# Who issues the small transfer of row maxima: ScalarE's queue or the sync queue

## The reference, cut to what matters

```python
q = heads(x @ Wq + bq); k = heads(c @ Wk + bk); v = heads(c @ Wv + bv)   # 16 heads of 16 channels
att = softmax(q @ k.T / sqrt(16))            # 512 x 512 for every head
y   = att @ v
```

## Time and profile before

| | |
|---|---|
| median of 3 runs | 1839.13 us (1838.22 to 1843.45) |
| span of the profiled execution, first to last instruction | 1831.7 us |
| what lies around the span, against the median | 7.4 us |
| PE busy | 1634.0 us, 89% |
| DVE busy | 1353.5 us, 74% |
| ACT busy | 1151.3 us, 63% |
| POOL busy | 658.3 us, 36% |
| q1 (SP's queue) | 156.43 MB, 30.8% of the 16 DMA engines' time |
| q10 (ACT's queue) | 1.18 MB, 0.3% |

### The profile page before, as it was taken

One profiled execution on the slowest core, in us unless ns is written; L12 is line 12 of the kernel. 1 busy time (PEld: TensorE's weight loads), 2 busy tenths in 40 slices (PEclk: granted clock), 3 DMA queues, 4 the chain that ended last, 5 costly groups with the idle time before them and its releaser, 6 DMA issues.

```text
span 1831.7 us, 29160 instructions
## 1 busy us (share of the span) xinstructions
PE 1634.0 (89%) x10051; PEld 735.1 (40%) x10064; DVE 1353.5 (74%) x2549; ACT 1151.3 (63%) x2178; POOL 658.3 (36%) x915
## 2 busy tenths in 40 slices
PE   5897879998999989998999999988999998899677
PEld 1343335433543435433543344433543543333236
DVE  6677677788588777778687777877488687688287
ACT  1474576566755686667765685657655854756497
POOL 3422524550445234641454135622562242310140
PEclk7898989999999999999999999999999998899899
DMA  7333412323243323332242323332332231124123
GB/s 196 101 108 108 121 35 72 99 79 90 63 117 79 93 59 99 88 101 67 67 113 62 91 77 92 86 102 76 82 105 59 54 102 47 44 77 138 46 70 116
DMA packets 106947, 159.49 MB, mean 87 GB/s; under 512 B 20656, under 2 KB 83248, under 8 KB 106800
## 3 DMA queue, kind: packets, MB, share of 16 engines
q1 hardware_dynamic: 101904, 156.43, 30.8%
q10 hardware_dynamic: 4896, 1.18, 0.3%
HBM read 105.00 MB, written 51.38 MB: 85 GB/s over the span
## 4 chain that ended last, share of the span: by engine, by line
PE 54%; DVE 19%; ACT 10%; POOL 7%; issue 4%; DMA 3%; SPq 1%; ACTq 0%; DVEq 0%; POOLq 0%
PE acc L1492 11%; PE st L1478 10%; PE misc L1457 10%; DVE nmax L1255 8%; PE misc L1432 7%; PE misc L1404 4%; PE misc L1519 3%; PE misc L1444 3%; ACT probs L988 3%; ACT tail_h L1058 2%; ACT tail_h L1043 1%; PE misc L1546 1%; PE misc L1533 1%; POOL parts L873 1%; POOL qk L869 1%
## 5 line engine op out<-in xcount | busy, mean ns | idle before, releaser
L1255 DVE TENSOR_REDUCE nmax<-misc 128x1 f32<-128x512 f32 (+2 forms) x1376 | 863.8, 671 | 301.9 <-PE misc L1457 181.4
L988 ACT ACTIVATE probs<-st 128x512 f32<-128x512 f32 (+3 forms) x1536 | 760.4, 551 | 375.2 <-PE st L1478 241.3
L1457 PE MATMUL misc<-stack 96*128 96x512 bf16 (+3 forms) x1536 | 535.1, 364 | 58.2 <-DVE nmax L1255 41.1
L1478 PE MATMUL st<-stack 99*128 99x512 bf16 (+3 forms) x1536 | 539.8, 362 | 37.6 <-ACT probs L988 31.5
L1478 PEld LDWEIGHTS st<-stack 99*128 99x128 bf16 x1536 | 148.7, 98 | 377.8 <-ACT probs L988 222.0
L1457 PEld LDWEIGHTS misc<-stack 96*128 96x128 bf16 x1536 | 151.9, 99 | 199.1 <-DVE nmax L1255 83.1
L1492 PE MATMUL acc<-probs,v_x 128*32 128x512 f32 x1152 | 157.8, 621 | 0.0
L867 POOL TENSOR_TENSOR parts<-qk,zero 128x512 bf16<-128x512 f32 x78 | 81.3, 1043 | 207.6 <-ACT qk L971 207.6
L879 POOL TENSOR_TENSOR nparts<-nmax,zero 128x16 bf16<-128x16 f32 x96 | 21.3, 222 | 273.3 <-DVE nmax L1255 273.3
L1492 PE MATMUL acc<-probs,v_s 128*32 128x512 f32 (+3 forms) x1152 | 113.6, 466 | 0.1
L1481 PE MATMUL st<-mask_st,identb 128*128 128x128 bf16 x512 | 111.1, 220 | 0.0
(11 more groups left out here) (258 smaller groups left out, 2087.2 us busy)
## 6 DMA issues: line engine op xcount, KB each, us to landing
parts_xk<-parts SPq DMA_DIRECT2D x54, 128.0 KB
parts_xq<-parts SPq DMA_DIRECT2D x54, 128.0 KB
stack<-parts_xq SPq DMA_DIRECT2D x36, 192.0 KB, 3.2
stack<-parts_xk SPq DMA_DIRECT2D x36, 192.0 KB, 3.7
parts_sk<-parts SPq DMA_DIRECT2D x48, 128.0 KB
parts_sq<-parts SPq DMA_DIRECT2D x48, 128.0 KB
stack<-parts_sq SPq DMA_DIRECT2D x32, 192.0 KB, 2.9
stack<-parts_sk SPq DMA_DIRECT2D x32, 192.0 KB, 3.4
```

The costliest lines, as they stand in the source:

```text
L988: act.activation(probs[:, j % P_SLOTS, c, T - w:], st_bank(n, 4 * j + c)[:, 0:w], ACT.Exp, scale=SCALE).then_inc(exp_done, 1)
L1255: dve.tensor_reduce(nmax[:, ring, first:first + NT * (len(cs) - 1) + 1:NT], src, AX.X, ALU.max, negate=True).then_inc(misc_free[slot], 1)
L1457: last = pe.matmul(o, stack[0:ROWS, r, 0, c, P * i:P * i + P], stack[0:ROWS, r, 1, c, 0:w], start=True, stop=not causal)
L1478: last = pe.matmul(o[:, 0:w], stack[0:AUG, r, 1, c, P * j:P * j + P], stack[0:AUG, r, 0, c, T - w:T], start=True, stop=not causal)
```

## The change

The issue of the 96 transfers moves from ACT's `negmax_T` to a new function of the same name on SP, which is entered in SP's walk. It waits for the same semaphore (the copy to `nrow` is done), moves the same bytes and counts up the same semaphore. No step of the list is moved: on SP the transfer takes the place that `negmax_T` has in the list. ACT keeps the copy and no longer waits for its end.

```diff
@@ sync
+            def negmax_T(s):
+                r = s.n.slot(2)
+                wait_misc_read(sp, s)
+                sp.dma_start(stack[ROWS:AUG, s.n.slot(STACKS), 0, :, :].rearrange("o c (i t) -> o (c i) t", i=NT),
+                             nrow[:, r, :]).then_inc(negmax_landed[r], 16)
+
...
-                          stack=stack_, finish=finish_most))
+                          stack=stack_, negmax_T=negmax_T, finish=finish_most))
@@ scalar, negmax_T
                 copy_misc(s, 0, nrow[:, r, :], lambda b: as_bf16(b)[0:PARTS * HU * NT, 0:P])
-                wait_misc_read(act, s)
-                act.dma_start(stack[ROWS:AUG, s.n.slot(STACKS), 0, :, :].rearrange("o c (i t) -> o (c i) t", i=NT),
-                              nrow[:, r, :]).then_inc(negmax_landed[r], 16)
```

## The result

The changed kernel takes 1862.4 us in the median of 4 runs (1859.96 to 1866.48) against 1838.7 for the kernel before: ratio 1.014, 95% interval 1.0108 to 1.0172, so 20 to 32 us slower. The profiled execution has a span of 1861.3 us, 29.6 more than that of before. The forecast was 1875 us, +36. Direction and mechanism hold. The waits came out a little smaller than forecast, and ACT's freed time was worth more.

The account below looks back on a forecast made before the run. In-order PE, 89% busy and 54% of the chain, was taken as the bound. Net stalls +47.8, less 5 for ACT, 3.5 at the start and 3.3 near the end, gave +36: 1875 us, 8 in 10 from 1846 to 1900.

Parts of the forecast that it names:

- What bounds it, and SP's order: Whole kernel: in-order PE bounds it; SP, following its list, reaches `negmax_T` too late in five of a turn's 12 units.
- Landing of 2.6 us after SP's issue: Transfers behind SP's writes: they land 2.6 us after those writes end; range 2.5 to 3.3 us.
- The rival with 3.3 us: Landings behind writes or stores take 3.3 us and nothing is recovered: +68, 1907 us; chance 0.15.
- Sum of the stalls: PE's first `scores` of late units, all turns: stalls of 38.0 + 11.7 + 2.5 + 7.6 = 59.8 us.
- load_mid: Unit behind the 512 KB load on SP: transfer lands 0.4 us after it, 2.5 us stall; 0.5 if it overtakes.
- 20% of the stalls recovered: Behind PE's stalls: later waits for DVE and ACT shrink, taking back 12 us; net 47.8 us; ends none and half.
- the second rival: PE's 11% idle time absorbs most stalls, leaving some 12 of 60 us, cancelled by gains: 1839 us; chance 0.12.
- Start and end: First transfer and those near the end meet less bulk traffic on SP's queue: gains of 3.5 and 3.3 us.
- Tail loads, and the cost of the 96 issues on SP: Seven tail loads start some 1702 instead of 1682.87, covered by 19 us; SP's 70 us of issues hidden: no cost.
- ACT's 5 us: ACT freed of 96 issues of 729 ns, 70 us: 5 us gained on the path; bounds nothing and 12.
- The third rival: ACT's time counts for 20 of 70 us and SP's lateness is harmless: 1812 us; chance 0.11.
- half of the stalls with overtaking and 12 us for ACT: Fast end of the forecast's own range: half the stalls recovered, overtaking at `load_mid`, ACT worth 12 us; given as 1848 us.

Follow-up runs that it names:

- sp_ahead: Changed kernel, but on SP alone each `negmax_T` goes one step ahead of a `project`, `load_mid` or `finish` before it: 1821.3 us, ratio 0.9912 to the kernel before.
- changed_hold_full: Changed kernel plus a second, unused transfer of the true shape issued by ACT in all 96 units: 1871.5 us, ratio 1.0198 to the kernel before.
- changed_2: The changed kernel measured once more, nothing altered, as base for the run with ACT held: 1861.9 us, ratio 1.0142 to the kernel before.
- late_act: Against the changed kernel, ACT issues the 44 transfers behind `project`, `load_mid` or `finish`, SP the other 52: 1817.8 us, ratio 0.9894 to the kernel before.
- sp_ahead_2: The program of sp_ahead measured again, as base for the same kernel with ACT held: 1815.1 us, ratio 0.9871 to the kernel before.

## Why the prediction came out as it did, step by step

- *What bounds it, and SP's order:* right, and shown by sp_ahead. DVE waits longer for PE, as forecast.
- *Landing of 2.6 us after SP's issue:* right, 2.55 to 2.88 us behind writes in the turn shown. The rival with 3.3 us falls.
- *Sum of the stalls:* 59.8 us in 33 places forecast, 52.8 in 32 measured. The term that was off is `load_mid`: 2.5 us in each of five turns forecast, 12.5 in all; measured 1.16, 1.26, 1.25 and 1.48 in the four like turns and none in the turn before them, 5.2 in all. The landing was late as said (4.30 us), but SP came to it earlier than the old trace let expect: the stall one unit ahead moved ACT's copy back and SP's loads less, so that the issue stood 1.9 us behind the copy instead of 2.9. Here a stall took from the next one.
- *20% of the stalls recovered:* about right. In time, changed_hold_full is 36 us above the kernel before; with the 7 us of the two ends added back, lateness costs 43 us out of 52.8, so 18% is recovered (net 47.8 us forecast). Through the table it is 40 to 50 us, so between 5% and 25%. PE's idle time in the profiles says it without PE's slower stretches: 214.0 and 217.1 us in the two of the changed kernel against 176.3 and 176.1 in those of sp_ahead, 38 to 41 us for 51 us of waits, and 220.7 against 183.6 with ACT held, 37 for 49. So 19% to 26% is recovered. Where, the prediction said, and the lines of sp_ahead and the changed kernel show it: PE waits less for DVE and ACT.

```profile
PE misc L1480 <- DVE nmax L1278: 38.0, 35, 5.0
PE st L1501 <- ACT probs L1011: 28.1, 32, 3.6
```

```profile
PE misc L1460 <- DVE nmax L1258: 31.0, 34, 5.0
PE st L1481 <- ACT probs L991: 24.8, 29, 2.1
```

That most of the stalls are absorbed, the second rival, falls.

- *Start and end:* 6.8 us forecast, 7 measured. By the traces the start gave 54.37 - 50.25 = 4.1 us (3.5 forecast) and the end 1.9 (3.3 forecast): just ahead of the wait near 1690 the changed kernel's `scores` are 31.7 us behind those of before, and 29.9 behind from the last unit on.
- *Tail loads, and the cost of the 96 issues on SP:* right, hidden. PE's longest wait for a stack load is 12.5 us before and after.
- *ACT's 5 us:* too small in time, the second term that was mis-sized. Holding ACT again cost 10 us in the changed kernel, which is inside the stated bounds (nothing and 12), and 12 to 20 with the order right, more than "the chain gives ACT's issues under 9 us". PE's idle time explains some 7 us of the latter; in the changed kernel it is 4 to 7 us longer with ACT held (220.7 against 217.1 and 214.0). The chain is one path, and work close behind it isn't in its shares; that this is why it gave too little is argued, not shown. The line "ACT probs <- ACT nrow 12.2, 15" counts exponentials that wait for the copy, not those that start late because the issue holds the engine. The third rival had a true half, ACT's time; its other half, lateness without harm, is false.
- *What the forecast had no term for:* PE's longer busy time at the lower clock, 13.3 us between the profiles of before and after, but 5.2 between before and changed_2 (1634.0 against 1639.2 us, clocks 0.957 and 0.954). The stalls were priced as idle time alone. That 18% recovered in time came so near the 20% taken is in part luck.

The sum with measured terms is 43 - 7 - 10 = +26 us; forecast 47.8 - 6.8 - 5 = +36. So about 5 of the 10 us between them lie in the lateness, where `load_mid` was too dear, and 5 in ACT. The +26 is no test of the terms: the 43 and the 10 are both taken from changed_hold_full, and the 26 is what changed_2 itself measured (24 in the first measurement). One slip in the prediction's working: half of the stalls with overtaking and 12 us for ACT come to 1839 + 24.9 - 12 - 6.8 = 1845, not 1848; the stated range hardly changes by it.

The rule of the Trainium skill on ring order within a queue row ("DMA: Bandwidth & Descriptors", "Queues, rings and completion order") fits the 4.30 us at `load_mid` against some 2.6 elsewhere, and its price was under half of what the prediction made of it. No run has the same transfer beside the same 512 KB on a queue of its own, so that the order within the row is the cause isn't shown. The Trainium skill's rule that issuing from several engines only saves the issue time ("Trainium Kernel Development and Optimization", "Key Constraints") agrees with ACT's gain, 10 to 20 us here. What cost more in this case is SP's own place in line, as sp_ahead shows.

Both kernels are beaten by sp_ahead (ratios 0.9912 and 0.9871) and late_act (0.9894), that is, by the same move made with the order kept right.

## What to carry to other kernels

Before an issue is moved to another queue, find for each instance when that queue gets to it: the end of the step ahead in its own order, plus the landing, against the moment at which the consumer wants it. An engine whose queue looks idle may be idle because it waits, as SP is here, and what stands behind such a wait is late; then move the issue ahead of the wait too. And price an engine's issue time by holding the engine and measuring base and test together: its share of the chain can be too low.

## What was not expected of the hardware

The same kernel had profiled spans 15 us apart, with a lower granted TensorE clock in the longer one. The spans of sp_ahead and sp_ahead_2 (one program):

```profile
core 0: 1808.8 us, clock 0.956
```

```profile
core 0: 1824.2 us, clock 0.948
```

PE's idle time in the two is the same (176.3 and 176.1 us); its busy time is 1632.5 and 1648.1 us. So for this program PE's idle time repeats better than the span does.

In the changed kernel PE idled for 2.57 us ahead of 548.17, and a stretch at 1.2 GHz followed. Busy time by stretch there (us, then each engine's busy us and instructions, clock, DMA share, GB/s):

```profile
540.00:549.00 9.00, 6.43 (x49) 2.76 (x47) 5.08 (x9) 3.50 (x11) 7.59 (x8) 1.00 0.15 45
549.20:552.60 3.40, 3.40 (x7) 1.54 (x6) 1.73 (x3) 1.20 (x3) 0.65 (x3) 0.50 0.45 129
552.60:556.00 3.40, 3.40 (x27) 1.75 (x26) 2.03 (x4) 2.54 (x6) 1.89 (x2) 1.00 0.86 221
```

7 matmuls in 3.4 us against 27 in the next 3.4, though not of one kind. The kernel before had such a stretch later in the turn, where PE had waited too:

```profile
590.00:593.40 3.40, 2.14 (x11) 0.52 (x7) 3.37 (x9) 1.76 (x4) 0.00 (x0) 1.00 0.96 233
593.50:596.90 3.40, 3.38 (x4) 1.32 (x5) 1.17 (x2) 0.07 (x1) 0.00 (x0) 0.50 0.24 51
```

In this turn the slow stretch of before (593.50 on) has no match in the changed kernel, whose clock is 1.00 from 590 to 612, and that of the changed kernel (549.20 on) has none before, where the clock is 1.00 from 540 to 556. So slow stretches lie elsewhere after the change, and a stall may cost or give back more than its own length; which stall moves which stretch was not isolated. The profiled runs have mean clocks of 0.957 before and 0.949 and 0.954 in the two of the changed kernel. By PE's busy time 13 and 5 us of the longer spans go with that; how much of the 24 us is clock stays open. The other finding is the price of an issue: 729 ns on ACT for 48 rows of SBUF into three partitions, 309 ns for the same bytes into DRAM, and 760 ns on SP for the former.
